# Set-up of a fused two-phase kernel: two load groups, head weights padded by the host, shared keys inside the second pass

## The chip, the cores and the metric

The kernel runs on one core of a Trainium2 chip. The metric is the device time of one execution in microseconds (us), the median of several runs. Three runs of the kernel before gave 2236.84, 2244.34 and 2247.42 us; the median is 2244.34 us.

## The reference

There are 16 batches. Each batch has 196 patch tokens (a 224 x 224 image in 16 x 16 patches, multiplied by a weight to 192 channels) and 128 text tokens, 324 tokens in all. What is computed, cut to what matters:

```
h  = patches @ W_tok, joined with txt               # 324 x 192
h += FourierAttention(LN(h))                        # softmax over tokens, circular correlation, W_V, W_proj
h += gelu(LN(h) @ in_weight.T + in_bias) @ out_weight
xt = concat(LN(h), sc_token)                        # 196 shared tokens, the same in every batch
h += softmax(q k^T / 4) v @ W_proj + b_proj         # 12 heads of 16, 324 queries, 520 keys
x5 = LN(...); probs = softmax(x5 @ w_router.T)      # 4 experts, top 162 tokens each
y  = per expert masked w1; gelu MLP + own attention, w2 in two layers that are summed
out = h + gated sum
```

The keys and values of the 196 shared tokens do not depend on the batch, so they are computed once. The last weight, `w2`, comes as two layers of 192 outputs; the kernel uses only their sum, which is also made once.

## The kernel before

**Phases.** A first phase takes every batch up to the router's probabilities. Then one routing step works on all batches. A second phase does the expert layers. Each phase is a software pipeline: `iteration` (L364) walks a fixed order table, `ORDER_1` or `ORDER_2`, and each word in it is a step. `s` is one score matmul with its exponential, `a` one sum over values, `m` one maximum, `r` the row of maxima. The named steps are the other stages: `tok` is the patch matmul, `ln1` to `ln4` the layernorms, `t1` to `t5` the transposes, `hid` and `out` the MLP, `qk` and `v` the projections for the attention, `todram` and `pack` the rearrangement of queries and keys through DRAM. `OFF_1` gives each step the batch it works on, relative to the pass number `i`. The first phase runs passes i = -2 to 16, of which 1 to 12 are a loop on the chip and the others are written out (`loops`, L393).

**Order of work.** Each engine walks the same table and does its own part of each step. Semaphores order the engines. PSUM banks go round in rings (`Ring`, L110): `lin` with two banks, `mps` with three. When a step has no batch in a pass, it is skipped, but its place in the ring still has to be counted. In `skip` (L122) TensorE waits for the last two or three users of the bank, waits for its own count and increments it (L130). The scalar or vector engine does one wait and one increment (L134). In pass i = -2 the first step with a batch is `tok.0`, in the seventh line of `ORDER_1`; ahead of it stand 31 `m`, one `r` and 14 uses of `lin`.

**Set-up before the first pass.** SyncE primes the semaphores and then issues all loads on one queue (L459 to L474). The weights of the head projections, `w_p1` and the two layers of `w_2a`, are loaded by head: 12 heads times 3 transfers, since each head's 16 rows go to partitions 32 apart. POOL clears `w_p1` and `w_2a` first, because the rows between are not loaded. The second layer of `w_2` goes to `g` and that of `w_2a` to `av`; the vector engine adds them (L814 to L818). All engines wait for all loads. TensorE then makes the shared keys and values (L1102 to L1111); the keys are cut into three bf16 pieces by the scalar engine, the vector engine and POOL, written to DRAM (`scr_k`) and read back six times into `kpack` (L478 to L486). TensorE waits for these (L1114). POOL issues the first batch's `x` and text (L611) only after its part of the pieces and all loads.

Of the kernel before, what the change touches and what calls it, by code (L numbers as in the profile page):

```python
# [5 lines left out]
B = 16  # L6
IMG, TXT, SC = 196, 128, 196
N = IMG + TXT
C = 192
# [87 lines left out]
class Signal:  # L97
# [4 lines left out]
    def __init__(self, sem, per, primed=1, first=0):  # L102
        self.sem, self.per, self.primed, self.first = sem, per, primed, first
# [6 lines left out]
class Ring:  # L110
# [54 lines left out]
class Attention:  # L165


    def __init__(self, name, kt, rows, halves, values, order, offsets, lin, mps, signal, first):
# [5 lines left out]
        self.items, self.parts, lin_uses, mps_uses = [], {}, [], []  # L174
        n, m = 0, 0
        for slot, words in enumerate(order):
# [25 lines left out]
        self.mps = Ring(name + "_mps", mps, mps_uses, signal, first)  # L202
        self.scored = signal(name + "_scored", self.units)
# [21 lines left out]
def build(nc, A):  # L225
# [3 lines left out]
    with ctx:  # L229
# [134 lines left out]
        def iteration(eng, who, i, att, quad, sums, maxima, rows, step):  # L364


            for kind, what, part in att.items:
# [7 lines left out]
                elif kind == "m":  # L375
                    q, n = what
                    if has(att.batch(i, q), 0, B - 1):
                        maxima(att, i, q, n)
                    else:
                        att.mps.skip(eng, who, i, ("m", q, n))  # L380
# [12 lines left out]
        def loops(eng, run, second):  # L393
# [11 lines left out]
        loads, setup_dve, setup_pe, setup_act, setup_pool, sc_first, sc_rest, sc_mid, sc_pieces, sc_scr, sc_pack = (  # L405
            signal(n, 0) for n in ("loads", "setup_dve", "setup_pe", "setup_act", "setup_pool", "sc_first",
# [33 lines left out]
        SETUP_POOL, SETUP_DVE = 12, 11  # L440
        block = ctx.enter_context(nc.Block())

        LOADS = [
            (w_tok, A["w_tok"]), (w_a, A["w_a"]), (w_v0, A["w_v0"]), (w_p0, A["w_p0"]),
            (w_in, A["w_in"]), (b_in, A["b_in"]), (w_out, A["w_out"]), (w_qkv, A["w_qkv"]),
            (w_r, A["w_r"]), (gamma, A["gamma"]), (beta, A["beta"]), (w_1, A["w_1"]),
            (ident, A["ident"]), (dft, A["dft"]), (idft, A["idft"]),
            (cum, A["cum"]), (cum8, A["cum8"])]
        NLOAD = len(LOADS) + 2 + 3 * H + 3 + 1
# [6 lines left out]
        def _(sp):  # L456
            for s in primed:
                sp.sem_inc(s.sem, s.at(s.first, 0))
            for dst, src in LOADS:  # L459
                sp.dma_start(dst.ap(), src).then_inc(loads.sem, 16)  # L460
            sp.dma_start(w_2[:, :, :], A["w_2"][:, 0]).then_inc(loads.sem, 16)
            sp.dma_start(g[:, :, 0:C], A["w_2"][:, 1]).then_inc(loads.sem, 16)

            sp.wait_ge(setup_pool.sem, 2)
# [6 lines left out]
            sp.dma_start(b_p0[:, :], A["b_p0"].partition_broadcast(P)).then_inc(loads.sem, 16)  # L471
            sp.dma_start(b_p1[:, :], A["b_p1"].partition_broadcast(P)).then_inc(loads.sem, 16)
            sp.dma_start(b_2[:, :, :], A["b_2"].partition_broadcast(P)).then_inc(loads.sem, 16)
            sp.dma_start(xS[0:KC, :, N:NK1], A["sc"]).then_inc(loads.sem, 16)  # L474
            sp.wait_ge(setup_dve.sem, SETUP_DVE)
            sp.wait_ge(setup_pool.sem, SETUP_POOL)

            sp.wait_ge(sc_pieces.sem, 2)  # L478
            for m in range(2):
                sp.dma_start(scr_k[:, 128 * m:128 * m + SCK[m], 0:SC].rearrange("s p n -> p s n"),  # L480
                             piece[0:SCK[m], m, :, 0:SC]).then_inc(sc_scr.sem, 16)
            sp.wait_ge(sc_scr.sem, 32)
            for r, s in enumerate(K_PARTS):
                sp.dma_start(kpack[r * D:(r + 1) * D, :, N:NK1],
                             scr_k[s, :, 0:SC].rearrange("(d h) n -> d h n", d=D)).then_inc(sc_pack.sem, 16)
            sp.wait_ge(sc_pack.sem, 16 * 6)  # L486
# [43 lines left out]
            def first_step(name, k, c, what, j, i):  # L530
                if name == "todram":
# [56 lines left out]
        def _(pool):  # L588
            for n, (x, value) in enumerate(((w_p1[:, :, :], 0.0), (w_2a[:, :, :], 0.0), (xS[KC:KP, :, :], 0.0),
                                            (v1[:, :, :, :], 0.0), (kpack[KC:KP, :, :], 0.0),  # L590
                                            (yA[KC:KP, :, :], 0.0), (v1[:, 0:KT1 - 1, :, D:D + 1], 1.0),
                                            (v1[0:LAST1, KT1 - 1, :, D:D + 1], 1.0),
                                            (kpack[6 * D:6 * D + 3, :, :], 1.0),
                                            (yA[KC:KC + 1, :, :], 1.0), (of[64:KP, :, :, :], 0.0), (bc[:, :, :], 1.0))):
                if n:
                    pool.wait_ge(setup_pool.sem, n)
                nc.gpsimd.memset(x, value).then_inc(setup_pool.sem, 1)
            for m, p in enumerate(SCK):
                pool.wait_ge(sc_rest.sem, m + 1)
                nc.gpsimd.tensor_copy(piece[0:p, m, 1, 0:SC], rest[0:p, m, 0:SC]).then_inc(sc_mid.sem, 1)  # L600
                pool.wait_ge(sc_mid.sem, m + 1)
                nc.gpsimd.tensor_tensor(piece[0:p, m, 2, 0:SC], rest[0:p, m, 0:SC], piece[0:p, m, 1, 0:SC],
                                        ALU.subtract).then_inc(sc_pieces.sem, 1)
            pool.wait_ge(loads.sem, 16 * NLOAD)

# [5 lines left out]
            load_x(0)  # L611

# [10 lines left out]
            def first_step(name, k, c, what, j, i):  # L623
                if name == "xload":
# [23 lines left out]
                elif name == "hb":  # L648

                    front.emptied(pool, i - 1, "proj_1")  # L650
# [24 lines left out]
        def _(act):  # L675
            act.wait_ge(loads.sem, 16 * NLOAD)
            act.wait_ge(setup_dve.sem, SETUP_DVE)

            for m, p in enumerate(SCK):
                act.wait_ge(setup_pe.sem, m + 1)  # L680
                nc.scalar.copy(piece[0:p, m, 0, 0:SC], lin[0:p, m, 0:SC]).then_inc(sc_first.sem, 1)
            act.wait_ge(setup_pool.sem, SETUP_POOL)
            for m, p in enumerate((TK1, LAST1)):
                act.wait_ge(setup_pe.sem, m + 3)
                nc.scalar.copy(v1[0:p, KT1 - 2 + m, :, 0:D],
                               mps[0:p, m, 0:C].rearrange("p (h d) -> p h d", d=D)).then_inc(setup_act.sem, 1)
# [11 lines left out]
            def first_parts(att, ring, j, i, what, m):  # L698
                ring.filled(act, i, what)
                act.wait_ge(att.scr_in.sem, att.scr_in.at(j, 0))  # L700
# [16 lines left out]
            def first_step(name, k, c, what, j, i):  # L717
                if c != one.parts[what] - 1:
# [57 lines left out]
            def quad(att, i, n):  # L776
                act.wait_ge(att.scored.sem, att.scored.at(i, n + 1))
# [24 lines left out]
            loops(act, lambda i: iteration(act, "act", i, one, quad, sums, nothing, rows, first_step), False)  # L802
# [3 lines left out]
        def _(dve):  # L806

            for x in (xT1[KC:KP, :, :], xT2[KC:KP, :, :], aT[KC:KP, :, :], vz[KC:KP, :, :], cntb[:, :, :],
                      qpack[KC:KP, :, :], prob[KC:KP, :, :]):
                nc.vector.memset(x, 0.0).then_inc(setup_dve.sem, 1)  # L810
            dve.wait_ge(loads.sem, 16 * NLOAD)
            nc.vector.tensor_copy(identb[:, :], ident[:, :]).then_inc(setup_dve.sem, 1)

            nc.vector.tensor_tensor(w_2[:, :, :], w_2[:, :, :], g[:, :, 0:C], ALU.add).then_inc(setup_dve.sem, 1)  # L814
            for r in range(0, 128, 32):
                done = nc.vector.tensor_tensor(w_2a[r:r + D], w_2a[r:r + D], av[r:r + D, :, 0:C], ALU.add)
            done.then_inc(setup_dve.sem, 1)
            nc.vector.tensor_tensor(b_2[:, 0], b_2[:, 0], b_2[:, 1], ALU.add).then_inc(setup_dve.sem, 1)  # L818
            for m, p in enumerate(SCK):
                dve.wait_ge(sc_first.sem, m + 1)  # L820
# [576 lines left out]
```

## Time and profile before

| | us |
|---|---|
| median of three runs | 2244.34 |
| the profiled execution | 2232.77 |
| its span, first to last instruction | 2231.1 |
| TensorE (PE) busy | 1903.3 (85%) |
| vector engine (DVE) busy | 1416.2 (63%) |
| scalar engine (ACT) busy | 1109.0 (50%) |
| GpSimd (POOL) busy | 260.7 (12%) |

The profile is of one execution. Its time is longer than its span by what lies before the first and after the last instruction. Busy times leave out waits and the issuing of DMAs. The shares are averages over the whole span: the opening, where hardly anything is busy on TensorE, weighs little in them, so the opening has to be read in a view of its own. In the rows below PE is TensorE's matmul, PEld its weight load, DVE the vector engine, ACT the scalar engine, POOL GpSimd, and SPq the queue of DMAs that SyncE issues. A clock of 1.00 is 2.4 GHz on TensorE, 0.50 is 1.2 GHz.

### The profile page before, as it was taken

What the parts mean: (1) busy time and instruction counts of PE and PEld (TensorE: products, weight loads), DVE (VectorE), ACT (ScalarE), POOL (GpSimd) and SP (SyncE); (2) the same over time, 40 slices, a digit from 0 to 9 for tenths busy, and PEclk for the clock granted to TensorE, in tenths of its full rate; (3) what the DMA queues carried; (4) which work ended last, traced back from release to release, by engine and by line L of the source; (5) the groups of instructions that cost most, each with busy time, mean ns of one, the idle gap of its engine ahead of it and who ended that gap; (6) DMA issues with size and microseconds to landing.
All of it is one profiled execution on the core that took longest, in us unless ns stands there. A gap on an engine that the chain in (4) does not pass through costs nothing. (4 is left out here: it accounts for less than half of the span.)

```text
span 2231.1 us, 45808 instructions
## 1 busy us (share of the span) xinstructions
PE 1903.3 (85%) x11896; PEld 1275.0 (57%) x11896; DVE 1416.2 (63%) x4501; ACT 1109.0 (50%) x2577; POOL 260.7 (12%) x404
## 2 busy tenths in 40 slices
PE   0368899889999999989999988832999999999996
PEld 0245566566666666656656655421666666666664
DVE  2236677677678677777777766524566656656663
ACT  0024545545545545545545554410656656666663
POOL 3010010011011011011011001000010100100100
PEclk9679999999999999999999998855999999999998
DMA  4020220221221121121022021002243343333431
GB/s 135 14 53 1 59 56 25 58 54 33 49 54 42 40 62 44 35 59 54 24 60 57 20 59 50 26 24 67 64 117 90 95 103 95 101 91 99 116 81 34
DMA packets 157284, 133.82 MB, mean 60 GB/s; under 512 B 31760, under 2 KB 136480, under 8 KB 157088
## 3 DMA queue, kind: packets, MB, share of 16 engines
q1 hardware_dynamic: 153472, 127.46, 21.8%
q0 software_dynamic: 2304, 4.79, 0.8%
q10 hardware_dynamic: 1440, 0.75, 0.1%
q8 instruction: 33, 0.54, 0.1%
q14 instruction: 35, 0.29, 0.0%
HBM read 81.52 MB, written 50.16 MB: 59 GB/s over the span
## 5 line engine op out<-in xcount | busy, mean ns | idle before, releaser
L1018 DVE TENSOR_REDUCE mxh<-mps 108x1 f32<-108x260 f32 (+1 forms) x1728 | 683.2, 443 | 344.6 <-PE mps L1179 333.1
L780 ACT ACTIVATE prob<-sps 108x324 f32<-108x324 f32 x1536 | 624.6, 440 | 501.3 <-PE sps L1157 455.9
L1157 PE MATMUL sps<-qpack,kpack 128*108 128x324 bf16 x1536 | 445.9, 326 | 34.4 <-ACT prob L780 27.9
L1179 PE MATMUL mps<-kpack,qpack 96*108 96x260 bf16 (+1 forms) x1728 | 415.6, 297 | 45.5 <-DMA kpack<-scr_k 26.8
L1179 PEld LDWEIGHTS mps<-kpack,qpack 96*108 96x108 bf16 x1728 | 220.0, 130 | 192.2 <-DVE mxh L1018 77.2
L1170 PE MATMUL aps<-prob,v 128*32 128x324 f32 x3072 | 324.2, 466 | 3.1 <-PEq L130 2.3
L1157 PEld LDWEIGHTS sps<-qpack,kpack 128*108 128x108 bf16 x1536 | 193.3, 130 | 221.9 <-ACT prob L780 162.6
L1147 PE MATMUL lin<-yT,w 128*128 128x324 f32 x576 | 183.5, 452 | 8.3 <-DVE yT L1063 7.6
L618 POOL CAST piece<-rest 128x324 bf16<-128x324 f32 x96 | 43.7, 456 | 782.0 <-DVE rest L889 769.1
L1170 PEld LDWEIGHTS aps<-prob,v 128*32 128x32 f32 x3072 | 74.4, 110 | 105.0 <-issue 56.4
L1147 PEld LDWEIGHTS lin<-yT,w 128*128 128x128 f32 x576 | 103.6, 193 | 51.8 <-issue 11.7
L1147 PE MATMUL lin<-xT,w_in 128*128 128x324 f32 x384 | 119.7, 445 | 0.6 <-ACT xT L691 0.6
L634 POOL TENSOR_TENSOR hx<-ha,xna 108x576 f32<-108x576 f32 x16 | 22.4, 1400 | 828.8 <-DVE xna L863 828.8
L1137 PE MATMUL lin<-w_out,g 128*108 128x192 f32 x576 | 107.6, 328 | 1.8 <-PEq L130 1.8
L1137 PE MATMUL lin<-w,g 128*108 128x192 f32 x576 | 107.7, 328 | 0.0
L1120 PE MATMUL lin<-ident,xn 108*96 108x108 f32 x384 | 66.8, 300 | 38.5 <-DVE xn L863 30.5
L701 ACT CAST piece<-lin 128x324 bf16<-128x324 f32 x96 | 41.3, 430 | 113.4 <-PE lin L1147 111.7
L1137 PEld LDWEIGHTS lin<-w_out,g 128*108 128x108 f32 x576 | 91.6, 175 | 4.0 <-issue 2.3
L1137 PEld LDWEIGHTS lin<-w,g 128*108 128x108 f32 x576 | 91.2, 173 | 2.5
L695 ACT ACT_TABLE_LOAD x62 | 79.5, 1283 | 21.6 <-PE lin L1147 20.5
L792 ACT COPY av<-aps 128x324 f32<-128x324 f32 x96 | 41.2, 429 | 96.5 <-PE aps L1170 71.3
L889 DVE TENSOR_TENSOR rest<-lin,piece 128x324 f32<-128x324 f32 x96 | 47.6, 496 | 61.2 <-ACT piece L701 32.8
(156 smaller groups left out, 2445.3 us busy)
## 6 DMA issues: line engine op xcount, KB each, us to landing
qpack<-scr_q SPq DMA_DIRECT2D x96, 243.0 KB, 3.3
kpack<-scr_k SPq DMA_DIRECT2D x96, 121.5 KB, 3.4
scr_q<-piece SPq DMA_DIRECT2D x32, 243.0 KB, 2.9
scr_k<-piece SPq DMA_DIRECT2D x32, 243.0 KB, 3.6
kpack<-scr_k SPq DMA_DIRECT2D x96, 81.0 KB, 3.2
bc<-rec_d SPq DMA_DIRECT2D x128, 60.8 KB, 2.3
scr_q<-piece SPq DMA_DIRECT2D x32, 162.0 KB, 3.2
scr_q<-piece SPq DMA_DIRECT2D x64, 81.0 KB, 3.1
```

Of the source, the lines that this page charges most:

```text
L618: nc.gpsimd.tensor_copy(piece[:, m, 1, :], rest[:, m, :]).then_inc(att.second.sem, 1)
L695: nc.scalar.activation(g[:, f, :], ring.at(what)[:, 0:N], ACT.Gelu, bias=b_in[:, f:f + 1] if bias else 0.0).then_inc(ring.free["act"].sem, 1)
L701: nc.scalar.copy(piece[:, m, 0, :], ring.at(what)[:, 0:N]).then_inc(att.first.sem, 1)
L780: nc.scalar.activation(prob[0:rows, n % NP, :], sps[0:rows, n % 2, 0:N], ACT.Exp, scale=SCALE).then_inc(att.exped.sem, 1)
L889: nc.vector.tensor_tensor(rest[:, m, :], ring.at(what)[:, 0:N], piece[:, m, 0, :], ALU.subtract).then_inc(ring.free["dve"].sem, 1)
L1018: nc.vector.tensor_reduce(mxh[:, hd, t, s:s + 1], att.mps.at(use)[0:P, 0:att.width], AX.X, ALU.max, negate=True).then_inc(att.mps.free["dv ...
L1120: done = nc.tensor.transpose(b[0:KC, t * P:(t + 1) * P], src[:, t, k * KC:(k + 1) * KC], ident[0:P, 0:P])
L1137: done = mm(tiles2(b)[0:P, t % 2, :], acts[k][:, t * P:(t + 1) * P], weights[k], start=k == 0, stop=k == 5)
L1147: done = mm(b[0:size, 0:N], w[:, k, c:c + size], x[:, k, 0:N], start=k == 0, stop=k == 1)
L1157: mm(sps[0:rows, n % 2, 0:N], kpack[:, 4 * q + n % 4, k * att.rows:k * att.rows + rows], qpack[:, 4 * q + n % 4, :], start=True, stop=True ...
L1170: mm(aps[32 * hd:32 * hd + 32, 0:N], att.values[:, k, 4 * q + hd, :], prob[:, n % NP, :], start=k == 0, stop=k == kt - 1).then_inc(att.sum ...
L1179: mm(bank[0:P, 0:att.width], qpack[0:6 * D, 4 * q + hd, t * P:(t + 1) * P], kpack[0:6 * D, 4 * q + hd, s * att.width:(s + 1) * att.width], ...
```

## The change

1. **Two load groups.** Seven weights and `b_p0`, which pass i = -2 uses, are loaded first and counted on `loads_first`. The others follow on `loads`. TensorE waits for the first group before pass -2, and TensorE and the scalar engine wait for the second between passes -2 and -1.
2. **Head weights padded by the host.** `w_p1` and both layers of `w_2a` come from the host with 32 rows a head, so each is one transfer. The two memsets that cleared them go.
3. **First batch first.** POOL issues the load of batch 0 before its memsets.
4. **Skipped steps.** Each engine leaves out, in the first pass of each phase, the items of the table ahead of the first step with a batch. The primed semaphores start at the counts those items would have left.
5. **Shared keys in pass -1.** A step `shared` stands behind `hid2` in `ORDER_1` and runs in pass i = -1 only. The matmuls write `mps` and `sps` instead of `lin` and `mps`.
6. **Weight sums on POOL.** The second layers are loaded into `prob`; in `shared`, behind the pieces, POOL adds them, adds the bias layers, and clears `prob`'s lower partitions.
7. Waits are added at the first use: `sc_scr` and `sc_pieces` at batch 0's pieces, `shared_in` at the first maximum, `SETUP_POOL` at the first score.

```diff
-    "m hid2 hid3 s m s m hid4 m m norm a m",
+    "m hid2 shared hid3 s m s m hid4 m m norm a m",
...
+    def passed(self, n):
+        self.full.passed = n
+        for e, s in self.free.items():
+            s.passed = self.uses[:n].count(e)
...
+                offset = offsets.get(step, offsets.get(base(step)))
+                if self.begin is None and offset is not None and has(first + offset, 0, B - 1):
+                    self.begin, lin_passed, mps_passed = len(self.items), len(lin_uses), len(mps_uses)
...
+                if isinstance(i, int) and i == att.first_pass and n < att.begin:
+                    continue
...
+                elif what == "shared":
+                    if isinstance(i, int) and i == -1:
+                        step(what, 0, 0, what, None, i)
...
                 run(i)
+                if i == -2 and between:
+                    between()
...
+        FIRST = [(w_tok, A["w_tok"]), (ident, A["ident"]), (w_a, A["w_a"]), (w_v0, A["w_v0"]), (dft, A["dft"]),
+                 (idft, A["idft"]), (w_p0, A["w_p0"])]
         LOADS = [
+            (w_in, A["w_in"]), (b_in, A["b_in"]), (w_qkv, A["w_qkv"]), (w_out, A["w_out"]),
+            (w_r, A["w_r"]), (gamma, A["gamma"]), (beta, A["beta"]), (w_p1, A["w_p1"]), (w_1, A["w_1"]),
             (cum, A["cum"]), (cum8, A["cum8"])]
...
-            for hd in range(H):
-                r = 32 * (hd % 4)
-                sp.dma_start(w_p1[r:r + D, hd // 4, :], A["w_p1"][hd * D:(hd + 1) * D, :]).then_inc(loads.sem, 16)
-                for s, dst in enumerate((w_2a, av[:, :, 0:C])):
-                    sp.dma_start(dst[r:r + D, hd // 4, :],
-                                 A["w_2a"][s, hd * D:(hd + 1) * D, :]).then_inc(loads.sem, 16)
...
+            sp.dma_start(w_2s, A["w_2"][:, 1]).then_inc(loads.sem, 16)
+            sp.dma_start(w_2a[:, :, :], A["w_2a"][0]).then_inc(loads.sem, 16)
+            sp.dma_start(w_2as, A["w_2a"][1]).then_inc(loads.sem, 16)
...
             load_x(0)
+            for n, (x, value) in enumerate(((of[64:KP, :, :, :], 0.0), (xS[KC:KP, :, :], 0.0), (v1[:, :, :, :], 0.0),
...
+            def both_layers():
+                pool.wait_ge(loads.sem, 16 * NLOAD)
+                nc.gpsimd.tensor_tensor(w_2[:, :, :], w_2[:, :, :], w_2s, ALU.add).then_inc(setup_pool.sem, 1)
+                nc.gpsimd.tensor_tensor(w_2a[:, :, :], w_2a[:, :, :], w_2as, ALU.add).then_inc(setup_pool.sem, 1)
+                nc.gpsimd.tensor_tensor(b_2[:, 0], b_2[:, 0], b_2[:, 1], ALU.add).then_inc(setup_pool.sem, 1)
+                pool.wait_ge(setup_pool.sem, SETUP_POOL - 1)
+                nc.gpsimd.memset(prob[KC:KP, :, :], 0.0).then_inc(setup_pool.sem, 1)
...
-            act.wait_ge(loads.sem, 16 * NLOAD)
-            act.wait_ge(setup_dve.sem, SETUP_DVE)
...
-            pe.wait_ge(loads.sem, 16 * NLOAD)
-            pe.wait_ge(setup_dve.sem, SETUP_DVE)
-            pe.wait_ge(setup_pool.sem, SETUP_POOL)
+            pe.wait_ge(loads_first.sem, 16 * NFIRST)
+            pe.wait_ge(setup_dve.sem, SETUP_DVE - 1)
+            pe.wait_ge(setup_pool.sem, 1)
...
+                        done = mm(mps[0:p, m, 0:SC], w_qkv[:, k, C + m * 128:C + m * 128 + p], xS[:, k, N:NK1],
+                                  start=k == 0, stop=k == 1)
...
+                        done = mm(sps[0:p, m, 0:C], xS[:, k, N + m * TK1:N + m * TK1 + p], w_qkv[:, k, 2 * C:],
+                                  start=k == 0, stop=k == 1)
```

## Rows read from the trace of the kernel before

**Rows 1.** The page's head: span and number of instructions.
```profile
span 2231.1 us, 45808 instructions
```
**Rows 2.** Waits up to 73 us: waiter, releaser, us in total, times, longest.
```profile
PE lin L1204 <- PEq L130: 21.9, 1, 21.9
...
PE lin L1104 <- DVE b L818: 45.3, 1, 45.3
```
**Rows 3.** Timeline of the set-up: start us, us, engine, line, operation, count.
```profile
4.99 0.42 SPq L460 DMA_DIRECT2D w_tok<-in_w_tok  x1
7.39 3.30 DVE L810 MEMSET prob<- 32x3888 f32 x1 [0.76 <-issue]
16.31 2.35 SPq L467 DMA_DIRECT2D w_p<-in_w_p  x1
...
36.21 0.68 SPq L474 DMA_DIRECT2D xS<-in_sc  x1
40.51 1.35 DVE L814 TENSOR_TENSOR w<-w,g 128x1152 f32<-128x1152 f32 x1
...
47.05 1.28 ACT L681 ACT_TABLE_LOAD   x1 [47.05 <-PE lin L1104]
48.34 0.53 ACT L681 CAST piece<-lin 128x196 bf16<-128x196 f32 x2
...
50.47 0.55 POOL L602 TENSOR_TENSOR piece<-rest,piece 64x196 bf16<-64x196 f32 x1
```
**Rows 4.** Stretches: length, busy PE PEld DVE ACT POOL, clock, DMA share, GB/s.
```profile
5.00:8.00 3.00, 0.00 (x0) 0.00 (x0) 2.24 (x2) 0.00 (x0) 3.00 (x1) 1.00 0.51 117
8.00:11.00 3.00, 0.00 (x0) 0.00 (x0) 2.68 (x1) 0.00 (x0) 2.88 (x3) 1.00 0.96 309
...
20.00:25.00 5.00, 0.00 (x0) 0.00 (x0) 0.00 (x0) 0.00 (x0) 0.00 (x0) 1.00 1.01 321
41.00:51.00 10.00, 5.49 (x16) 3.85 (x16) 4.75 (x8) 2.31 (x5) 1.72 (x5) 1.00 0.00 0
```
**Rows 5.** Line 484, reading the shared key pieces back: issues and landing.
```profile
L484 SPq DMA_DIRECT2D kpack<-scr_k x6: 602/603/605, 54.7 to 57.9; - x6
...
DMA to landing us min/median/max: 2.8/3.0/3.1
```
**Rows 6.** Timeline of passes -2 and -1.
```profile
72.70 2.87 PE L1204 MATMUL lin<-w_tok,pT 128*108 128x192 f32 x8 [21.91 <-PEq L130]
...
78.23 0.17 DVE L852 TENSOR_SCALAR var<-mv 108x3 f32<-108x3 f32 x1
...
80.55 0.96 DVE L863 TENSOR_SCALAR xn<-hin,mv,rs 108x192 f32<-108x192 f32 x3
...
82.99 1.29 PE L1120 MATMUL lin<-ident,xn 108*96 108x108 f32 x6 [7.42 <-PEq L130]
...
114.77 8.59 PE L1147 MATMUL lin<-xT,w_in 128*128 128x324 f32 x24 [0.56 <-ACT xT L691]
...
118.14 4.70 PEld L1147 LDWEIGHTS lin<-xT,w_in 128*128 128x128 f32 x17 [0.20 <-issue]
...
129.35 0.56 DVE L882 TENSOR_TENSOR h<-lin,h 108x384 f32<-108x384 f32 x1 [16.57 <-PE lin L1137]
...
133.28 1.68 POOL L654 TENSOR_TENSOR hb<-hin,b_p 108x192 f32<-108x192 f32 x3 [49.51 <-ACTq L134]
133.32 0.57 DVE L852 TENSOR_SCALAR var<-mv 108x3 f32<-108x3 f32 x1
...
145.73 4.69 SPq L494 DMA_DIRECT2D scr_q<-piece  x5
```
**Rows 7.** The page's costly groups: busy us, mean ns, idle before.
```profile
L634 POOL TENSOR_TENSOR hx<-ha,xna 108x576 f32<-108x576 f32 x16 | 22.4, 1400 | 828.8 <-DVE xna L863 828.8
```
**Rows 8.** Two passes of the loop as stretches, columns as in rows 4.
```profile
543.00:625.00 82.00, 74.46 (x493) 51.01 (x491) 61.25 (x212) 43.31 (x103) 10.92 (x19) 0.98 0.18 46
625.00:707.00 82.00, 76.61 (x491) 51.65 (x491) 61.24 (x211) 43.49 (x103) 10.88 (x18) 0.94 0.18 46
```

More of the change, by code:

```diff
@@ L102, in __init__ @@
     def __init__(self, sem, per, primed=1, first=0):
-        self.sem, self.per, self.primed, self.first = sem, per, primed, first
+        self.sem, self.per, self.primed, self.first, self.passed = sem, per, primed, first, 0
     def at(self, i, n):
@@ L457, in _ @@
             for s in primed:
-                sp.sem_inc(s.sem, s.at(s.first, 0))
-            for dst, src in LOADS:
+                sp.sem_inc(s.sem, s.at(s.first, 0) + s.passed)
+            for dst, src in FIRST:
+                sp.dma_start(dst.ap(), src).then_inc(loads_first.sem, 16)
+            sp.dma_start(b_p0[:, :], A["b_p0"].partition_broadcast(P)).then_inc(loads_first.sem, 16)
+            for dst, src in LOADS[:4]:
+                sp.dma_start(dst.ap(), src).then_inc(loads.sem, 16)
@@ L475, in _ @@
[L475 to L485, printed above, removed]
@@ L588, in _ @@
         def _(pool):
[L589 to L604, printed above, removed]
             def load_x(j):
@@ L699, in first_parts @@
                 ring.filled(act, i, what)
+                if att is one and isinstance(j, int) and j == 0:
+                    act.wait_ge(sc_scr.sem, 32)
                 act.wait_ge(att.scr_in.sem, att.scr_in.at(j, 0))
@@ L776, in quad @@
             def quad(att, i, n):
+                if att is one and isinstance(i, int) and i == 0 and n == 0:
+                    act.wait_ge(setup_pool.sem, SETUP_POOL)
                 act.wait_ge(att.scored.sem, att.scored.at(i, n + 1))
@@ L800, in rows @@
                 act.dma_start(qpack[6 * D:6 * D + 3, 4 * q:4 * q + 4, :], mT[:, :]).then_inc(att.rows_in.sem, 16)
-            loops(act, lambda i: iteration(act, "act", i, one, quad, sums, nothing, rows, first_step), False)
+            loops(act, lambda i: iteration(act, "act", i, one, quad, sums, nothing, rows, first_step), False,
+                  lambda: act.wait_ge(loads.sem, 16 * NLOAD))
             loops(act, lambda i: iteration(act, "act", i, two, quad, sums, nothing, rows, second_step), True)
@@ L806, in _, with shared_keys @@
         def _(dve):
-            for x in (xT1[KC:KP, :, :], xT2[KC:KP, :, :], aT[KC:KP, :, :], vz[KC:KP, :, :], cntb[:, :, :],
-                      qpack[KC:KP, :, :], prob[KC:KP, :, :]):
+            for x in (xT1[KC:KP, :, :], aT[KC:KP, :, :], vz[KC:KP, :, :], xT2[KC:KP, :, :], qpack[KC:KP, :, :], cntb[:, :, :]):
                 nc.vector.memset(x, 0.0).then_inc(setup_dve.sem, 1)
[L811 to L820, printed above, removed]
-                nc.vector.tensor_tensor(rest[0:p, m, 0:SC], lin[0:p, m, 0:SC], piece[0:p, m, 0, 0:SC],
-                                        ALU.subtract).then_inc(sc_rest.sem, 1)
-            dve.wait_ge(sc_pieces.sem, 2)
-            dve.wait_ge(setup_dve.sem, SETUP_DVE)
+            dve.wait_ge(setup_dve.sem, SETUP_DVE - 1)
+            def shared_keys():
+                dve.wait_ge(loads_first.sem, 16 * NFIRST)
+                nc.vector.tensor_copy(identb[:, :], ident[:, :]).then_inc(setup_dve.sem, 1)
+                for m, p in enumerate(SCK):
+                    dve.wait_ge(sc_first.sem, m + 1)
+                    nc.vector.tensor_tensor(rest[0:p, m, 0:SC], mps[0:p, m, 0:SC], piece[0:p, m, 0, 0:SC],
+                                            ALU.subtract).then_inc(sc_rest.sem, 1)
             links = [0]
@@ L887, in rests @@
                 dve.wait_ge(att.first.sem, att.first.at(j, m + 1))
+                if att is one and isinstance(j, int) and j == 0:
+                    dve.wait_ge(sc_pieces.sem, 2)
                 dve.wait_ge(att.third.sem, att.third.at(j - 1, m + 1))
@@ L1153, in quad @@
                 rows = att.tile[k]
+                if n == 0 and att is one and isinstance(i, int) and i == 0:
+                    pe.wait_ge(setup_pool.sem, SETUP_POOL)
                 if n % (4 * kt) == 0:
@@ L1176, in maxima @@
                 if n == 0:
+                    if att is one and isinstance(i, int) and i == -1:
+                        shared_in()
                     pe.wait_ge(att.pack_in[q].sem, att.pack_in[q].at(att.batch(i, q), 64))
```

139 lines of the change are left out of this document (93 added, 46 removed).

## The prediction

> **What bounds the kernel now.** I read the page first, then the waits of the opening stretch, its timeline, the transfer rates there, the timeline of the first batch, and last the passes of the main loop. The span is 2231.1 us [rows 1]; the execution took 2232.77, so 1.67 us lie around it. The page's own chain of waits covers less than 1% and does not help. The change touches only what runs before and inside the two opening passes (i = -2 and i = -1); the looped passes keep their instructions. So the question is at what time the first batch's patch matmul (`tok`, L1204) starts, and what is put into the pass behind it. In the waits [rows 2] the reader is to see two idle stretches: TensorE idles 45.3 us until the last weight sum is done, and then another 21.9 us before `tok`, released by its own sequencer at L130, the `sem_inc` of a skipped step. `tok` starts at 72.70 [rows 6]. Everything before it is set-up.
>
> The 72.7 us divide so [rows 3]: loads are issued from 4.99 on; the per-head loads start at 16.31 and, being 36 at 0.42 us and some gap, push the last load (shared tokens) to 36.21; the vector engine, which waits for it, starts its first sum at 40.51, so it lands near 40.3. The weight sums end at 45.2 (the first takes 1.35). Shared keys and values follow: matmuls, pieces (last one ends at 51.0), two transfers to DRAM, six back. The last of the six is issued at 57.9 and they land in 3.0 us [rows 5], so at about 60.9. Then nothing is seen on any engine until 72.7: 11.8 us. By the order table, 31 maxima and one row step stand ahead of `tok.0`, each skipped by TensorE with 3 + 1 waits and an increment, and 14 uses of the `lin` banks with 2 + 1 waits and an increment: 32 x 5 + 14 x 4 = 216 instructions, 55 ns each. The same rate shows behind `tok`: 18 x 5 + 11 x 4 = 134 skipped instructions fill the 7.4 us until the transposes at 82.99 [rows 6]; 55 ns again.
>
> **The change, part by part.**
>
> *Loads in two groups.* TensorE now waits for eight transfers, one vector set-up count and one memset of POOL. From the tile shapes the eight hold 192 + 64 + 12 + 192 + 492 + 324 + 192 + 81 KB = 1.59 MB. The stretches before moved 0.35 MB by 8 us and then 309 GB/s [rows 4], so 1.59 MB are through at 8 + 1.24/0.309 = 12.0 us. I add 2 us for the last completion, of the 3.0 us that one small transfer takes from issue to landing [rows 5]: 14.0 us. The bounds: 12.0 if the completion costs nothing; 27 if the engines serve the second group beside the first, since the rate stays at 321 GB/s until 25 [rows 4] and the host padding adds 0.43 MB, 1.4 us. I take 14.0, as the group is issued first and the trace's rate holds from 8 us on. The first batch's own three transfers leave POOL at about 1 us instead of 50.97 and find the engines idle. The six vector memsets that are waited for end before 7.4, where the one of `prob` began [rows 3], and POOL's first one takes under 1 us.
>
> *The skipped steps ahead of `tok`.* They are counted into the primed semaphores and issued no longer: 216 x 55 ns = 11.8 us off TensorE. Together with the loads, the sums, the shared keys and their round trip, `tok` moves from 72.7 to 14.0: 58.7 us. In the order of this sum: 40.3 to 14.0 for the loads (26.3), 45.2 - 40.3 = 4.9 for the sums, 60.9 - 45.2 = 15.7 for the shared chain, 11.8 for the skips. The second phase also starts its table later, at `scale0`, past some 8 maxima; there TensorE waits for DMA anyway. I take nothing, with 0 to 2 us less as bounds (some 40 skipped instructions at 55 ns).
>
> *The table load.* The scalar engine's first instruction is now the copy behind `tok`, so the table load of 1.28 us [rows 3] falls there. The layernorm ends at 81.51 and the transposes start at 82.99, held by the 134 skipped instructions and not by the layernorm [rows 6]; the cover is 1.4 us, so this costs 0. Without the cover it would be 1.3.
>
> In the rows the load takes 1.28 us and the cast starts 0.01 us behind its end. The Trainium skill (ScalarE: Activation LUTs, "What ACT_TABLE_LOAD costs") adds a drain of about 1.4 us to each switch. By that rule the step would cost 1.2 us more and the sum 1.2 less; this trace's rows show no such drain.
>
> *Pass i = -2* keeps its work: from `tok` at 72.7 to the transposes behind `ln2`, and then the first hidden matmul at 114.77 [rows 6]. POOL's memsets end near 20 (the old ones at 19.1, two of them are gone and three issues of x, 1.8 us, stand ahead), and `hb` is wanted by the projection 34 us behind `tok`, at 48: hidden.
>
> *Second group of loads.* 18 transfers behind the 8, 26 instead of 59 in all; issued by about 20, all bytes through by 27 at the rate above. They are wanted at 114 - 58.7 = 55: hidden by 28 us. Without that cover each microsecond of lateness would count in full.
>
> *Shared keys in pass -1.* TensorE gets the same 16 matmul records between `hid2` and `hid3`. They took 5.49 us at the start [rows 4]. In the hidden stage the weight loads come 0.28 us apart from 118.14 on (17 in 4.70 us) [rows 6], and 0.54 apart before it; the granted clock goes from 1.2 to 2.4 GHz there. `hid2` ends near 119.7, behind the rise. So the price is 5.49/2 = 2.75 us, between 0 (idle time behind `hid5` takes it up) and 5.5 (slow clock). I take 2.75, for TensorE is busy through this stage. What queues behind it is the rest of `hid`, then `out`. The scalar engine's four copies (0.32 each) and the vector engine's two subtractions and the `identb` copy lie in its waits for TensorE.
>
> *Pieces and weight sums on POOL.* The pieces take 2 us. Then three sums and the memset of `prob`: POOL adds 108 x 576 in 1.40 us [rows 7], so 1152 columns are 2.8 and 576 are 1.4; 192 columns are 0.56 by `hb`'s 1.68 for three [rows 6]; the memset 3.3 as on the vector engine [rows 3]. That is 8.1 us; POOL would be free at about 132 in old time. Its next work, `hb`, comes at 133.28, now 136 [rows 6]; hidden by 4 us. Were it late, the next x load would be, which starts 20 us behind. The vector engine's `out` residual stands at 129.35, now 132.1: just behind POOL's end. Bounds 0 to 2 us.
>
> On the vector engine the same sum of 1152 columns took 1.35 us, against my 2.8 on POOL. The Trainium skill (GPSIMD Engine Reference, "1. Specifications") adds that POOL shares its SBUF interfaces with the vector engine and that they contend. The trace agrees: beside `hb` on POOL the vector engine's addition of 108 x 3 took 0.57 us, against 0.17 at 78.23 [rows 6]. By that the `out` residual and the layernorm behind it would be stretched if POOL runs late, 1 to 2 us on the sum.
>
> *SyncE's part* now blocks its queue from the last piece for the length seen before, 60.9 - 51.0 = 10 us, to about 135. Behind it on SP is the write of batch 0's query pieces, at 145.73, now 148.5 [rows 6]: hidden by 13 us. The first maxima wait for it too, and they come after that. The added single waits (`sc_scr`, `sc_pieces`, `SETUP_POOL`) are all met by then.
>
> **Sum.** -58.7 + 2.75 + 0 = -55.9 us, so 2232.77 - 55.9 = 2176.9 for the profiled execution. That execution is the fastest of those shown; the median is 2244.34, 11.6 above it. The change takes off fixed work, so I take the difference from the median: 2188.4.
>
> **Rivals.**
> A. *The first group lands with the second.* Then `tok` starts at up to 27 instead of 14: +11 to 13, 2200. For it: all ride one queue at full rate [rows 4]. Against it: the order of issue.
> B. *The 11.8 us are not skipped steps* but code or something else that TensorE waits for; then they come back: 2200. Against it: 216 instructions at the rate of the 134.
> C. *The shared step holds pass -1 as a chain*: matmuls, pieces, DRAM and back stay in line, 15.7 us instead of 2.75: +13, 2201. Against it: SP's and POOL's slack of 13 and 4 us.
> D. *Slower.* The opening passes shift the loop against the clock's changes, and the passes get a lower granted clock. A loop pass takes 82 us at 0.98 with 74.5 us of TensorE busy, and 82 us at 0.94 with 76.6 [rows 8]: 2.1 us of busy time per 0.04, all taken up by idle time. The 5.4 us left at 0.94 are used up at 0.84; to eat 55.9 us over 13 looped and near-looped passes (4.3 each) the clock has to fall to 0.76 in each. Then 2245 or more. Neither of the two passes shown is near that. It decides at a loop clock of 0.76.
>
> **How the numbers follow.** Forecast 0.72; A 0.09, B 0.05, C 0.06; other losses of the gain 0.03; D or anything that lets no gain stand 0.05 (0.025 within 0.5%, 0.025 slower). 0.5% (11 us) is about what a measurement of this kernel can tell from no change. The runs shown spread over 2236.84 to 2247.42, so a median of three can lie 7 us below and 3 above mine; `tok` at 12.0 and an `out` stage that absorbs the shared matmuls give 5 less; so the low end is 2176. The high end takes in A to C with a little on top: 2205. Faster by over 0.5%: 0.95, same 0.025, slower 0.025.
>
> **What would show it.** The first `tok` matmul at 13 to 16 us, with no idle time charged to L130 before it; at 25 or later A or B. From `tok` to the first hidden matmul 42 us as before. Between `hid2` and `hid3` 16 records in 2.7 us, and the first query write of SP 76 us behind `tok` instead of 73. The last loads landed before 30. POOL done with the sums before the second `hb`. Loop passes of 81 to 82 us. A loop pass longer by over 1 us, or `tok` later than 20, makes the forecast wrong.

## The result and the profile after

| | us |
|---|---|
| after, median of four runs | 2189.09 (2185.83 to 2193.78) |
| before, median of four runs beside it | 2243.9 (2236.84 to 2247.42) |
| ratio, 95% interval | 0.9761 (0.973 to 0.9793) |
| after, profiled execution and its span | 2193.78 and 2191.6 |

The kernel became 54.8 us faster by the medians. The profiled executions differ by only 39 us (2232.77 and 2193.78), since that of before was faster than the four timed beside it and that of after is the slowest of its four; one pair of traces can't be used to divide 55 us. So I took each kernel again (experiments below) and compare several traces.

The waits up to 30 us, as in [rows 2], and the timeline that answers to [rows 3] and [rows 6]. In both the first `tok` matmul is the row to find: it now waits for `b_p0` (`b_p` in the rows), the last transfer of the first group, until 15.4 us.

```profile
PE lin L1269 <- DMA b_p<-in_b_p: 15.4, 1, 15.4
...
PE lin L1178 <- PEq L136: 7.3, 1, 7.3
...
ACT L766 <- DMA hin<-in_txt: 5.1, 1, 5.1
```

```profile
5.11 1.28 ACT L766 ACT_TABLE_LOAD   x1 [5.11 <-DMA hin<-in_txt]
8.82 0.45 SPq L481 DMA_DIRECT2D b_p<-in_b_p  x1
...
15.36 2.90 PE L1269 MATMUL lin<-w_tok,pT 128*108 128x192 f32 x8 [15.36 <-DMA b_p<-in_b_p]
...
20.31 1.68 POOL L692 TENSOR_TENSOR hb<-hin,b_p 108x192 f32<-108x192 f32 x3
25.54 1.28 PE L1178 MATMUL lin<-ident,xn 108*96 108x108 f32 x6 [7.29 <-PEq L136]
...
59.23 6.44 PE L1205 MATMUL lin<-xT,w_in 128*128 128x324 f32 x12 [0.51 <-ACT xT L728]
...
68.45 3.43 PE L1205 MATMUL lin<-xT,w_in 128*128 128x324 f32 x12
69.01 2.62 POOL L638 TENSOR_TENSOR w<-w,prob 128x1152 f32<-128x1152 f32 x1
73.59 3.33 POOL L642 MEMSET prob<- 32x3888 f32 x1
73.89 6.07 PE L1195 MATMUL lin<-w_out,g 128*108 128x192 f32 x36 [2.00 <-PEq L136]
78.05 0.56 DVE L923 TENSOR_TENSOR h<-lin,h 108x384 f32<-108x384 f32 x1 [10.17 <-PE lin L1195]
82.06 1.68 POOL L692 TENSOR_TENSOR hb<-hin,b_p 108x192 f32<-108x192 f32 x3 [5.14 <-ACTq L140]
...
94.31 5.34 SPq L513 DMA_DIRECT2D scr_q<-piece  x6
```

`tok` moved by 57.3 us, and the transposes behind it still wait for the skipped instructions and not for the layernorm: the 10.2 us between them are those of before. POOL is done with the sums at 76.92 and idle for 5.1 us ahead of `hb`. The first hidden matmul comes 43.9 us behind `tok` (42.1 before), the first query write 79.0 (73.0 before). The clock accounts for part of both: the projection in pass -2 ran at 1.2 GHz (3.77 us for 2.20 before), and so did more of the hidden stage. The stretches of the hidden stage show it; columns as in [rows 4]:

```profile
60.00:63.00 3.00, 3.00 (x7) 1.95 (x6) 0.00 (x0) 1.01 (x2) 0.00 (x0) 0.50 0.00 0
63.00:66.00 3.00, 3.00 (x10) 2.04 (x8) 0.00 (x0) 0.83 (x2) 0.00 (x0) 0.65 0.00 0
66.00:69.00 3.00, 3.00 (x17) 2.24 (x16) 0.71 (x2) 1.50 (x5) 1.69 (x4) 1.00 0.00 0
```

The granted clock is 0.50, that is 1.2 GHz, until some 6 us behind the first hidden matmul and then 2.4 GHz; before, it rose 3.4 us behind it.

### The profile page after: what moved, and what is told of

Its sections match the earlier page's. It is cut to its first block and busy times, and to the rows that moved or that the text cites. A ratio compares the mean times of both kernels' runs of the same rounds, so it can differ in the third digit from the quotient of the medians.

```text
span 2191.6 us, 45608 instructions
## 1 busy us (share of the span) xinstructions
PE 1912.5 (87%) x11896; PEld 1281.0 (58%) x11896; DVE 1408.6 (64%) x4494; ACT 1107.8 (51%) x2577; POOL 267.0 (12%) x406
## 5 line engine op out<-in xcount | busy, mean ns | idle before, releaser
L1205 PEld LDWEIGHTS lin<-yT,w 128*128 128x128 f32 x576 | 103.7, 193 | 52.0 <-issue 11.8
```

Of the source, the lines that this page charges most:

```text
L1205: done = mm(b[0:size, 0:N], w[:, k, c:c + size], x[:, k, 0:N], start=k == 0, stop=k == 1)
```

## The experiments

Each trace is read at the same four marks: `tok`, the first hidden matmul, the first `hc` copy on POOL (the end of the opening), and the next three passes. "Rest" is from there to the last `acc2` copy (POOL's `COPY hc<-acc`). Marks and passes are of the one profiled execution, the last column is the median of all.

| | tok | hidden | first hc | three passes | rest | median us |
|---|---|---|---|---|---|---|
| before | 72.7 | 114.8 | 134.9 | 244.6 | 1826.9 | 2243.9 |
| before_b | 72.8 | 117.0 | 138.2 | 245.3 | 1837.2 | 2247.1 (one) |
| before_c | 73.4 | 114.9 | 134.8 | 245.2 | 1829.8 | 2235.69 (one) |
| after | 15.4 | 59.2 | 83.7 | 248.9 | 1834.0 | 2189.09 |
| again | 15.3 | 57.3 | 82.4 | 250.5 | 1827.2 | 2184.25 |
| skips_back | 27.5 | 72.4 | 96.9 | 249.6 | 1828.0 | 2199.62 |
| one_group | 32.5 | 75.3 | 99.7 | 246.6 | 1825.2 | 2198.58 |
| x_late | 28.1 | 69.7 | 94.6 | 249.6 | 1828.7 | 2197.8 |
| per_head | 15.3 | 57.6 | 82.7 | 246.9 | 1827.2 | 2184.51 |
| sums_dve | 15.5 | 58.2 | 85.7 | 246.4 | 1830.5 | 2185.7 |
| shared_early | 15.4 | 57.0 | 77.1 | 245.0 | 1825.8 | 2184.8 |
| tok_first | 5.5 | 54.8 | 79.4 | 249.1 | 1827.8 | 2179.74 |
| early_all | 5.3 | 52.5 | 72.9 | 250.6 | 1832.1 | 2182.86 |
| no_stall | 5.2 | 47.1 | 67.6 | 245.4 | 1827.7 | 2166.31 |

The kernel before ran beside every group: 2238.23 beside again, skips_back, one_group and x_late, 2239.83 beside per_head, sums_dve, shared_early and tok_first, 2242.95 beside early_all, and 2236.03 beside no_stall.

**again.** No edit.

> The changed kernel once more, for a second trace and a tighter time. Theory (fixed work taken off the opening): 2189 within 4 us, 55 us under the kernel before, first tok matmul at 15.4 us. Open in the first trace are 11 us that it lost against the kernel before behind pass -1, in two loop passes of 83 and 85 us and in the second phase. Theory: these passes vary from execution to execution, and another trace has them elsewhere. Rival: the new opening puts the loop's start into a bad phase; then passes 1 and 2 are again 83 us or longer.

2184.25 us, 54.0 under the kernel before; ratio 0.9753 (0.9733 to 0.9774). `tok` agrees with after, and the later marks agree to 2 us. The three passes were long again: 84.2, 83.9 and 82.4 here, 81.3, 83.1 and 84.5 in after. The first half of the theory holds. For the second half the rival's sign came, the first two passes both over 83 us, though the first was not long in after; it had to be tested on the kernel before.

**before_b and before_c.** The kernel before, for two more traces.

> The kernel before, for a second trace. In its first trace the three passes behind the first hc copy took 244.6 us; in the traces of the changed kernel and its variants they took 245 to 250.5. Theory (which passes are long depends on where a stretch at 1.2 GHz falls, and that varies): the three take 245 to 250 here too. Rival (the new opening costs 2 to 6 us in the first passes by itself): 244 to 245 again.

> The kernel before, for a third trace, to the same question: 245 to 250 us in the three passes behind the first hc copy by the theory, 244 to 245 by the rival.

245.3 and 245.2 us in the three passes; with the first trace 244.6. The theory said 245 to 250 and the rival 244 to 245, so by their bounds these two don't decide. Taken together the traces speak for the rival: three of the kernel before lie within 0.7 us, and of eleven with a changed opening nine lie between 246.4 and 250.6 and two (shared_early and no_stall) at 245.0 and 245.4. In no_stall the long pass is the fourth, 84.3 us, just behind the mark. The new opening gives back 3 us on the average of after, again, per_head and sums_dve (248.2 against 245.1). One such pass, the third of after, and its stretch behind the loads of the packed keys:

```profile
274.00:277.00 3.00, 1.79 (x10) 1.43 (x11) 1.10 (x3) 0.00 (x0) 0.00 (x0) 0.96 0.24 48
277.00:280.00 3.00, 3.00 (x17) 1.56 (x16) 1.64 (x5) 0.33 (x1) 0.00 (x0) 0.50 0.00 0
280.00:283.00 3.00, 3.00 (x21) 2.65 (x20) 1.87 (x6) 0.94 (x3) 0.00 (x0) 0.97 0.03 5
```

```profile
PE mps L1241 <- DMA kpack<-scr_k: 2.4, 1, 2.4
```

TensorE waits 2.4 us for the transfer, is busy for 1.8 of the 3 us of the first stretch, and then has 3 us at 1.2 GHz with its busy time full. The kernel before, in the same part of its third pass, keeps the clock at 1.00 and waits 1.0 us:

```profile
323.00:326.00 3.00, 2.37 (x16) 1.72 (x20) 1.41 (x4) 0.13 (x1) 0.00 (x0) 1.00 0.51 98
326.00:329.00 3.00, 3.00 (x25) 2.24 (x18) 2.53 (x8) 1.20 (x3) 0.00 (x0) 1.00 0.00 0
```

This is not the only form. In again, skips_back, x_late and sums_dve the first of the three passes took 83.9 to 84.4 us, and TensorE waited for no packed keys in it; it was busy 64.7 to 65.0 us there, against 61.3 to 63.2 in the kernel before. Why the new opening leads to these longer passes more often was not settled.

**skips_back.** The skipped steps are walked again.

```diff
-                if isinstance(i, int) and i == att.first_pass and n < att.begin:
-                    continue
-                sp.sem_inc(s.sem, s.at(s.first, 0) + s.passed)
+                sp.sem_inc(s.sem, s.at(s.first, 0))
```

> The changed kernel, but every engine walks the items ahead of the first step with a batch again, and the semaphores are primed without them. Theory: TensorE is ready for its 216 skipped instructions as soon as the first load group lands at 15.3 us, so tok comes 11.8 us later, at 27.1, and the time is 12 us longer, 2201. Rival (the 11.8 us of idle time were a wait on something else, or code): tok stays near 15.4 and the time at 2189.

`tok` at 27.5, released by the sequencer at L136 again; 12.2 us later than in again, 56 ns for each of the 216 instructions. 2199.62 us, 15.4 over again. By the first `hc` copy it is 14.5 us; 1.9 of them are the projection in pass -2, which ran at 1.2 GHz in this trace and not in that of again.

**one_group.** TensorE waits for both groups.

```diff
             pe.wait_ge(loads_first.sem, 16 * NFIRST)
+            pe.wait_ge(loads.sem, 16 * NLOAD)
```

> The changed kernel, with one wait more on TensorE: it waits for the second load group too before pass -2. Theory: the last load lands near 28 us, so tok comes 12 to 13 us later and the time is 2201 to 2202. Rival: the transfers of the two groups are served side by side, so the first group lands hardly before the second and the time grows by under 4 us.

`tok` at 32.5, 17.1 us later, and 2198.58 us, 14.3 over again. I had the landing of the last load at 28, and it is at 32.4. Its direction holds: the groups land 17 us apart, so the first is not held until the second is through. That the first transfers of the second group took no share of the engines ahead of 15.4 us isn't shown by this.

**x_late.** `load_x(0)` behind the memsets.

> The changed kernel, but POOL issues the load of batch 0 behind its memsets, not ahead of them. Theory: the memsets end at 18.5 us, issues and landing take 5 us, so tok comes at 23.5 to 24, 8 us later, and the time is 2197. Rival: x is not waited for at that place and the time stays.

`tok` at 28.1, 12.8 us later, and 2197.8 us, 13.5 over again; I had expected 8. The memsets end at 17.9 (I had 18.5), and the three transfers are issued at 18.2 to 20.0. But they are in the middle of the second load group:

```profile
L613 POOL DMA_DIRECT2D hin<-in_txt x1: 558/558/558, 19.4 to 19.4; - x1
...
DMA to landing us min/median/max: 8.4/8.4/8.4
```

The three took 7.2, 7.1 and 8.4 us from issue to landing; the same three, issued from 1.4 us on when the loads had not begun, took 2.7, 2.4 and 2.4 in after. A small transfer on another queue shares the engines with the bulk. So issuing x first is worth more in this kernel than the memsets' length.

**per_head.** The head weights are loaded by head again, at the end of the second group; POOL clears the two tiles first and adds the second layer in four pieces.

```diff
+            sp.wait_ge(setup_pool.sem, 3)
+            for hd in range(H):
+                r = 32 * (hd % 4)
+                sp.dma_start(w_p1[r:r + D, hd // 4, :], A["w_p1"][hd * D:(hd + 1) * D, :]).then_inc(loads.sem, 16)
+                for s, dst in enumerate((w_2a, w_2as)):
+                    sp.dma_start(dst[r:r + D, hd // 4, :],
+                                 A["w_2a"][s, hd * D:(hd + 1) * D, :]).then_inc(loads.sem, 16)
...
```

> The changed kernel with the head weights loaded by head again, 36 transfers at the end of the second group, cleared by two POOL memsets and summed in four pieces on POOL. Theory: the issues end at about 36 us and the loads have landed by 40; they are wanted at 57, so the padding is worth nothing by itself once the loads are in two groups: 2184 to 2188, as the changed kernel beside it. Rival: SyncE's queue or POOL's longer sums (some 5 us more) reach the critical path, and the time grows by 3 us or more.

2184.51 us, ratio 0.9752 (0.9735 to 0.9768), that of again. The last load is issued at 39.3 us, not at 36, and POOL is done at 78.9, still 2.2 us ahead of `hb`. The padding is worth nothing here; the two groups alone take the 36 transfers off the path.

**sums_dve.** The sums and the memset of `prob` on the vector engine.

```diff
-                nc.gpsimd.tensor_tensor(w_2[:, :, :], w_2[:, :, :], w_2s, ALU.add).then_inc(setup_pool.sem, 1)
...
+                dve.wait_ge(loads.sem, 16 * NLOAD)
+                nc.vector.tensor_tensor(w_2[:, :, :], w_2[:, :, :], w_2s, ALU.add).then_inc(setup_pool.sem, 1)
...
```

> The changed kernel with the weight sums and the memset of prob on the vector engine, behind its part of the shared keys, instead of on POOL. Theory: the vector engine idles there from 67.9 to 78.0 us and the four operations take 6.5 us, so nothing moves: 2184 to 2188. Rival (POOL's sums hold up the opening by contention): the out stage and the layernorm come 1 to 2 us earlier.

2185.7 us, ratio 0.9749 (0.9733 to 0.9766): no difference in time. The opening is not quicker, so POOL's sums are hidden as forecast; it is 2 to 3.4 us slower by the first `hc` copy. Two things show in the trace. The vector engine holds the counts that TensorE waits for in its skipped steps:

```profile
66.50 2.66 POOL L632 TENSOR_TENSOR piece<-rest,piece 128x196 bf16<-128x196 f32 x1
...
69.79 2.42 PE L1206 MATMUL lin<-xT,w_in 128*128 128x324 f32 x8 [1.16 <-DVEq L140]
```

and POOL's subtraction takes 2.66 us (0.55 in after) beside the vector engine's sums.

**shared_early.** The step `shared` in pass -2, behind `of`.

```diff
-    "m hid2 shared hid3 s m s m hid4 m m norm a m",
+    "m hid2 hid3 s m s m hid4 m m norm a m",
...
-    "m dft_1.1 s m of s a s",
+    "m dft_1.1 s m of shared s a s",
...
-                    if isinstance(i, int) and i == -1:
+                    if isinstance(i, int) and i == -2:
...
             def shared_keys():
+                weights_in()
                 for m, p in enumerate(SCK):
```

> The changed kernel with the step `shared` in pass -2 behind `of`, where TensorE idles 4 us for the vector engine, instead of between hid2 and hid3. Theory (the 16 records are on the path in pass -1 and would be hidden here): the shared step costs 0 to 1 us instead of 3, and TensorE has less idle time before the inverse transforms, so that it may keep the 2.4 GHz clock: 3 to 6 us less, 2180. Rival: the hidden stage absorbs the records already; then the time is the changed kernel's, or 2 us more where the vector engine's subtractions delay the inverse.

The opening agrees: the first `hc` copy is at 77.1, 5.3 us ahead of again, and the profiled execution took 2174.36 us. But the median of six runs is 2184.8 (2174.36 to 2189.05), so a gain of the whole time isn't shown. The 3 us of shared matmuls lie under `of`, and the inverse transforms behind run at 2.4 GHz. In after the clock is 0.50 there, and the same 16 records take 4.85 us:

```profile
41.58 0.76 PE L1306 MATMUL lin<-idft,of 128*96 128x162 f32 x4 [0.96 <-DVEq L140]
42.83 1.86 PE L1306 MATMUL lin<-idft,of 128*96 128x162 f32 x12 [0.49 <-PEq L136]
```

One surprise costs 2 us of it:

```profile
48.41 3.33 POOL L642 MEMSET prob<- 32x3888 f32 x1
49.38 0.31 DVE L891 BATCH_NORM_AGGREGATE mv<-st 108x2 f32<-108x6 f32 x3
49.73 2.04 DVE L893 TENSOR_SCALAR var<-mv 108x3 f32<-108x3 f32 x1
```

A TENSOR_SCALAR of three columns takes 2.04 us and ends when POOL's memset ends.

**tok_first.** `w_tok` has a semaphore of its own and is issued ahead of the priming.

```diff
...
+            sp.dma_start(w_tok.ap(), A["w_tok"]).then_inc(loads_tok.sem, 16)
             for s in primed:
...
-            pe.wait_ge(loads_first.sem, 16 * NFIRST)
+            pe.wait_ge(loads_tok.sem, 16)
...
                 elif name == "t1":
+                    if isinstance(i, int) and i == -2 and k == 0:
+                        pe.wait_ge(loads_first.sem, 16 * NFIRST)
...
```

> The changed kernel with w_tok on a semaphore of its own, issued ahead of the priming of the semaphores; TensorE waits for it alone before tok, and for the rest of the first group before the first transposes. Theory: tok starts when x has landed and the semaphores are primed, at 6 us instead of 15.4, the transposes follow 10.2 us later at 16.5, by when the first group (15.3) is in: 8 to 9 us less, 2177. Rival: the first group is late with the last transfer, or the transposes wait for something else; the gain is under 4 us.

2179.74 us, ratio 0.9725 (0.9709 to 0.9741). `tok` at 5.5 as expected, but the first hidden matmul is only 2.5 to 4.4 us earlier. The time is 4.8 us under per_head beside it, nearer to the rival's 4 than to the theory's 8 to 9. The cause: the transposes waited until 20.6 us for the layernorm, whose last three operations took 5.57 us; see the next run.

**early_all.** Both edits (`tok` ahead as in tok_first, `shared` in pass -2 as in shared_early); `shared` waits only for `w_qkv` and the shared tokens, which form a group of their own; the sums are a step `layers` behind `hid2`.

> The changed kernel with w_tok alone ahead of tok, issued before the priming; with the shared step in pass -2 behind `of`, where it waits for w_qkv and the shared tokens alone; and with the weight sums and the memset of prob kept behind hid2 in pass -1 (a new step `layers`, POOL only). Theory: tok at 5.5 us, the gains of the two parts add up in the opening: 10 us for tok and 5 for the shared step, plus the 2 us that the memset of prob held the vector engine in the run with the early step; the first hc copy comes at 66 to 68 us instead of 82 to 84, and the time is 2168 to 2173. Rival: what the loop gives back with the clock eats the second gain; 2174 to 2180.

2182.86 us, ratio 0.973 (0.971 to 0.975), outside both ranges. The first `hc` copy is at 72.9, not at 66 to 68. A mistake of mine is part of it: POOL has no other work between, so it ran `layers` straight behind the pieces, and the 2.03 us stall was still there. The larger part stands in the first layernorm:

```profile
13.28 5.29 POOL L623 MEMSET kpack<- 3x6240 bf16 x1
14.78 5.57 DVE L906 TENSOR_SCALAR xn<-hin,mv,rs 108x192 f32<-108x192 f32 x3
...
43.92 3.33 POOL L642 MEMSET prob<- 32x3888 f32 x1
45.25 2.03 DVE L895 TENSOR_SCALAR var<-mv 108x3 f32<-108x3 f32 x1
```

Three operations of 0.96 us together took 5.57 and ended 1.8 us behind the end of the memset.

**no_stall.** early_all with POOL's memsets moved off the layernorms.

```diff
-            for n, (x, value) in enumerate(((of[64:KP, :, :, :], 0.0), (xS[KC:KP, :, :], 0.0), (v1[:, :, :, :], 0.0),
+            for n, (x, value) in enumerate(((kpack[KC:KP, :, :], 0.0), (of[64:KP, :, :, :], 0.0), (xS[KC:KP, :, :], 0.0),
...
+                if n == 3:
+                    pool.wait_ge(ln1_done.sem, ln1_done.at(0, 1))
...
+                pool.wait_ge(ln2_done.sem, ln2_done.at(0, 1))
                 nc.gpsimd.memset(prob[KC:KP, :, :], 0.0).then_inc(setup_pool.sem, 1)
```

> The kernel of early_all with POOL's work moved off the layernorms: the long zero memset of kpack first, the memsets of kpack's three rows and of v1 held until the first layernorm is done, and the memset of prob held until the first ln2 is done. In early_all three TENSOR_SCALAR of the first layernorm took 5.57 us together (0.96 elsewhere) beside the three-row memset, and one of ln2 took 2.03 (0.17) beside that of prob. Theory (a POOL memset holds the vector engine's TENSOR_SCALAR until it ends): they take 0.96 and 0.17 again, the first transposes come at 15.5 to 16 us, held by TensorE's skipped instructions or by the first load group, in place of 20.6, the first hidden matmul at 45.5 to 47 in place of 52.5, and the time is 2177 to 2182, some 3 to 6 under early_all, as the loop's passes allow. Rival (these times come from the loads that land in the same stretch): the same TENSOR_SCALAR stay long.

2166.31 us (2163.05 to 2166.94), ratio 0.9685 (0.9668 to 0.9702): 69.7 us under the kernel before, some 15 more than the change itself. The operations have their length again, with the loads still landing at 266 GB/s from 11 to 14 us, so the rival falls. The transposes now wait for the first load group:

```profile
10.78 0.17 DVE L899 TENSOR_SCALAR var<-mv 108x3 f32<-108x3 f32 x1
13.09 0.96 DVE L910 TENSOR_SCALAR xn<-hin,mv,rs 108x192 f32<-108x192 f32 x3
14.18 5.29 POOL L626 MEMSET kpack<- 3x6240 bf16 x1 [3.81 <-DVE xn L910]
15.50 1.29 PE L1185 MATMUL lin<-ident,xn 108*96 108x108 f32 x6 [7.39 <-DMA b_p<-in_b_p]
```

The transposes came at 15.5 and the first hidden matmul at 47.1, as expected. The time is 11 us under my range. Of the 15.0 us between the two profiled executions only 5.3 lie in the opening. The next four passes took 2.7 us less than in early_all and all behind them 7.0 less, and no run here shows why; the rest varied by nearly as much within one kernel (1827.2 and 1834.0 in again and after). This is the fastest version found.

## Why the prediction was right

The forecast was 2188.4 and the measured time 2189.09. Of its own signs, the start of `tok`, the missing wait at the skipped steps and POOL's sums ahead of `hb` came as said. The last loads were to land before 30 and landed at 32.4, the query write came 79.0 and not 76 us behind `tok`, and "a loop pass longer by over 1 us" was its sign of being wrong and did come. So the path and the large terms were right, and some of the small ones were not.

**The start of `tok` (forecast 14.0, measured 15.4 and 15.3).** The step holds to 1.4 us. The first group's last transfer was issued at 8.82 and landed at 15.3; by the rates of its stretches 1.59 MB had moved at some 12.5 us. Whether the 3 us behind that are the completion (I allowed 2) or a share that the second group took isn't separated. That group landed later than I had it, as the loads ran at 314 GB/s from 8 to 20 us where those of before ran at 354. one_group settles rival A: the second group lands 17 us later.

**The skipped steps (forecast 11.8, measured 12.2).** skips_back brings them back and the sequencer's wait with them; rival B falls.

**The table load (forecast 0).** It did not even lie behind `tok`: the engine loaded the table at 5.11 us, before the copy had its data. The drain of about 1.4 us that the Trainium skill states (ScalarE: Activation LUTs, "What ACT_TABLE_LOAD costs") would have cost nothing either, for the copy came only at 18.29; no row here shows one.

**The shared keys in pass -1 (forecast 2.75).** From the first hidden matmul to the first `out` matmul it takes 13.6 us in again and 13.6 in per_head, against 10.4 before: 3.2 us. shared_early takes them away again. But that is not the whole price. In again and per_head the `out` stage behind took 7.75 us for the 6.07 of before and after, with a granted clock of 0.55 in part of it; in after the clock rose later in the hidden stage instead, for 1.1 us:

```profile
70.89 7.75 PE L1195 MATMUL lin<-w_out,g 128*108 128x192 f32 x36 [2.00 <-PEq L136]
...
72.00:75.00 3.00, 3.00 (x12) 2.88 (x11) 0.00 (x0) 0.00 (x0) 1.92 (x1) 0.55 0.39 77
75.00:78.00 3.00, 3.00 (x21) 3.00 (x20) 0.56 (x1) 0.00 (x0) 0.00 (x0) 1.00 0.07 17
```

These rows are of again. From the first hidden matmul to the first `hc` copy the three took 24.5 to 25.1 us, the three traces of the kernel before 19.9 to 21.2, and shared_early 20.1: 4.5 us on the means for the 2.75 of the sum, inside its bound of 5.5. The projection in pass -2, which cost after 1.6 us at 1.2 GHz, is no cost of the change: it was as slow in before_b (3.83 us) and not in again. Rival C is excluded: the chain through DRAM stood beside the MLP, and SyncE waited 17.3 us for the query pieces afterwards, not they for it.

**Second group, padding, POOL's sums (forecast 0 each).** per_head and sums_dve show no difference in time. The Trainium skill (GPSIMD Engine Reference, "1. Specifications") says that POOL shares its SBUF interfaces with the vector engine and that they contend when the vector instruction is in a 2-port mode or has two SBUF inputs. Where the change puts the sums, the vector engine has nothing to do, so it cost nothing in after; in shared_early and early_all the same memset cost 1.9 us. The trace agrees in part: a TENSOR_SCALAR was held by a memset (the profile doesn't show its mode), and the small TENSOR_TENSOR, with two SBUF inputs, kept their 0.16 us beside one. Contention mattered for the versions beyond the change, and more than I had priced it.

**The loop (forecast 0).** This step was off by 3 us: the first three passes got longer. Rival D had named the place, at eighteen times the size, but it priced a pass by its mean granted clock, and that does not tell: the third pass took 84.5 us at 0.98 in after and 81.8 at 0.98 before. What makes these passes longer is open (before_b and before_c above). As a rival for the sign D is gone: the loop's passes behind took 81 to 83 us in both kernels, but for the fourth of no_stall.

**The sum.** Opening: the first `hc` copy at 136.0 us on the mean of three traces before and 83.6 on that of after, again, per_head and sums_dve, so 52.4 us; given back 3.1 in the passes; the rest is 1.6 shorter, which is within its scatter (1826.9 to 1837.2 in the kernel before). That makes 51 by traces and 54.8 and 54.0 by medians, against the 55.9 forecast. The three profiled executions of before average 2238.5 us, under their medians, and the four of the changed kernel 2188.0, over theirs; that is the difference between 51 and 54. By the traces the forecast was 5 us too high: by 1.1 at `tok`, 2.5 from there to the first `hc` copy and 3.1 in the passes, against 1.6 too low in the rest. That the median came within 1.1 us of the forecast is therefore in part luck. Taking the difference from the median and not from the profiled execution was needed: 2176.9 would have been 12 us too low.

## What to carry to other kernels

Before pricing a faster set-up, find in the timeline what the first matmul waits for, one releaser after another, and count idle time of a sequencer as instructions: here 216 waits and increments of skipped steps cost 12 us and could be counted into the start values. Load in the order of use and issue the first data ahead of the bulk, not only ahead of its own engine's work. Once the opening is short, look at what POOL does beside the vector engine's short chains, and at where TensorE idles: the shared matmuls moved there took no time of their own, and the matmuls behind them ran at 2.4 GHz.

## What the runs showed of the hardware

- A POOL memset held the vector engine's TENSOR_SCALAR: 2.03 us for three columns (0.17 alone), 5.57 for three operations of 0.96 together, while the TENSOR_TENSOR of a few columns that ran beside the same memset kept their 0.16 us. Beside POOL's TENSOR_TENSOR `hb` they took 0.50 to 0.57. The other way, POOL's subtraction took 2.66 us (0.55 alone) beside vector sums of 1152 and 576 columns (1.34 and 0.75 us).
- Three small transfers issued on POOL's queue in the middle of the bulk loads took 7.1 to 8.4 us to land, the same three on idle engines 2.4 to 2.7.
- A sequencer's waits and increments that have nothing to wait for took 56 ns each: 216 of them held TensorE for 12.2 us.
- In the loop a wait of 2.4 us for a transfer was followed by 3 us at 1.2 GHz, and that pass took 84.5 us in place of 81.8; other passes were as long without such a wait.
